# A decoder layer in fp32: its first stages laid out by scan step and tiled by columns

## The reference, cut to what matters

```python
xB = jnp.einsum('bsd,de->sbe', x, Bm)
h_final, _ = jax.lax.scan(lambda h, u: (h @ A + u, None), h0, xB)      # 256 steps
h_proj = h_final @ W_imp.T
importance = softmax(einsum('bsd,bd->bs', x, h_proj))
token_pref = softmax(einsum('bsd,nd->bsn', x, W_router))
neuron_w = einsum('bs,bsn->bn', importance, token_pref)
neuron_w = neuron_w / (neuron_w.sum(-1, keepdims=True) + 1e-08)
shared_compress = einsum('bn,ndr->bdr', neuron_w, compress)
Q = einsum('bsd,bdr->bsr', x, shared_compress)
scores = einsum('bsr,nr->bsn', Q, K) / sqrt(128)
# then: top 8 of 8192 scores per token, gather of V rows, their weighted sum, layernorm;
# cross-attention (16 heads), layernorm; a switched expert layer, layernorm
```

## Time and profile before

| | us |
|---|---|
| median of 3 runs (lowest to highest) | 1506.57 (1502.82 to 1507.38) |
| the profiled execution: its own time | 1504.98 |
| its span, first to last instruction | 1503.1 |
| PE, DVE, ACT, POOL busy | 1384.4, 1077.7, 736.7, 728.4 |
| mean granted TensorE clock | 0.968 |

### The profile page before, as it was taken

One profiled execution on the slowest core, in us unless ns is written; L12 is line 12 of the kernel. 1 busy time (PEld: TensorE's weight loads), 2 busy tenths in 40 slices (PEclk: granted clock), 3 DMA queues, 4 the chain that ended last, 5 costly groups with the idle time before them and its releaser, 6 DMA issues.

```text
span 1503.1 us, 25372 instructions
## 1 busy us (share of the span) xinstructions
PE 1384.4 (92%) x9840; PEld 1009.9 (67%) x9840; DVE 1077.7 (72%) x1626; ACT 736.7 (49%) x1381; POOL 728.4 (48%) x1010
## 2 busy tenths in 40 slices
PE   6986859999999999999999999999999988568998
PEld 2631648586877778686868777786868667356765
DVE  2110899978888888879788888888797862037567
ACT  2213435555555564646555555646465532315455
POOL 4400223747465564656474655656565753530225
PEclk9988889999999999999999999999999999879999
DMA  7316211213121212222131212122221311152313
GB/s 267 117 57 199 60 46 53 65 53 96 46 71 50 68 50 71 65 67 70 51 96 48 70 50 68 50 73 65 64 60 55 82 36 31 35 192 87 114 61 124
DMA packets 66759, 115.82 MB, mean 77 GB/s; under 512 B 10576, under 2 KB 44240, under 8 KB 66512
## 3 DMA queue, kind: packets, MB, share of 16 engines
q1 hardware_dynamic: 49200, 63.69, 14.7%
q0 software_dynamic: 14848, 41.96, 9.4%
q10 hardware_dynamic: 2592, 8.56, 1.7%
HBM read 103.42 MB, written 10.75 MB: 76 GB/s over the span
## 4 chain that ended last, share of the span: by engine, by line
PE 80%; DVE 13%; DMA 3%; issue 2%; POOL 1%; ACT 1%; SPq 1%; POOLq 0%; DVEq 0%; ACTq 0%
PE proj_bank L355 38%; PE score_bank L355 28%; PE sim_bank L355 10%; DVE cand_idx L948 3%; DVE cand_val L947 3%; DVE x_sum L971 2%; PE score_bank L641 2%; DMA comp_stage<-in_comp 1%; PE sim_bank L641 1%; DVE dispatchedT L1085 1%; PE sim_bank L575 1%; POOL exp L1170 1%; POOL v_rows L1141 0%; PE sim_bank L465 0%; DMA x_pair<-x_scratch 0%
## 5 line engine op out<-in xcount | busy, mean ns | idle before, releaser
L1141 POOL DMA_INDIRECT v_rows<-in_V,top_idx x256 | 248.2, 970 | 299.8 <-DVE top_idx L961 217.6
L727 ACT COPY score_row<-score_bank 128x512 f32<-128x512 f32 x512 | 298.5, 588 | 175.5 <-PE score_bank L355 103.0
L947 DVE MAX8 cand_val<-score_row 128x8 f32<-128x2048 f32 x128 | 292.2, 2282 | 103.7 <-ACT score_row L727 103.7
L1170 POOL TENSOR_SCALAR exp<-exp,exp_bound 128x256 f32<-128x256 f32 x512 | 246.9, 499 | 143.4 <-ACT exp L739 142.7
L948 DVE FIND_INDEX8 cand_idx<-cand_val,score_row 128x8 uint32<-128x2048 f32 x128 | 292.5, 2285 | 0.0
L355 PE MATMUL score_bank<-keysT_hi,qT_hi 128*128 128x512 f32 x512 | 219.5, 429 | 26.0 <-ACT score_row L727 25.0
L355 PE MATMUL score_bank<-keysT_lo,qT_hi 128*128 128x512 f32 x512 | 205.5, 401 | 0.0
L355 PE MATMUL score_bank<-keysT_hi,qT_lo 128*128 128x512 f32 x512 | 205.4, 401 | 0.0
L739 ACT ACTIVATE exp<-sim_bank 128x512 f32<-128x512 f32 x256 | 139.0, 595 | 113.8 <-PE sim_bank L355 113.8
L355 PE MATMUL sim_bank<-qT_heads,kT 64*128 64x256 f32 x1024 | 145.8, 403 | 7.7 <-ACT exp L739 7.7
L971 DVE SCALAR_TENSOR_TENSOR x_sum<-v_rows,top_weight,x_sum 128x256 f32<-128x256 f32 x256 | 134.7, 526 | 13.4 <-DMA v_rows<-in_V,top_idx 4.3
(11 more groups left out here) (168 smaller groups left out, 2301.3 us busy)
## 6 DMA issues: line engine op xcount, KB each, us to landing
kT<-den_scratch SPq DMA_DIRECT2D x64, 256.0 KB, 4.0
comp_stage<-in_comp SPq DMA_DIRECT2D x32, 256.0 KB, 3.7
x_pair<-x_scratch SPq DMA_DIRECT2D x32, 256.0 KB, 2.8
f_quads<-in_f POOLq DMA_DIRECT2D x32, 256.0 KB, 5.2
stage<-in_KmT ACTq DMA_DIRECT2D x8, 512.0 KB, 4.5
xT_all_<-in_xT SPq DMA_DIRECT2D x4, 1024.0 KB, 9.8
xT_in<-in_xT SPq DMA_DIRECT2D x16, 256.0 KB, 3.7
x_sum<-in_x SPq DMA_DIRECT2D x32, 128.0 KB, 2.1
```

The source lines that it names most:

```text
L727: nc.scalar.copy(srow[n // PER % 2][:, i * CB:(i + 1) * CB], scb[n % 3]).then_inc(sem("score_evac"), 1)
L947: own(nc.vector.max(cv[:, tile, cs], srow[g % 2][:, :]))
L1141: pool.indirect_dma_start(out=vg[:, k, :], out_offset=None, in_=V_rows, in_offset=bass.IndirectOffsetOnAxis(ap=i8[:, tile, k:k + 1], axis=0))\
L1170: last = nc.gpsimd.tensor_scalar(ex[i % NEX][:, k, :], ex[i % NEX][:, k, :], ub[:, k, c:c + 1], E_LO, ALU.min, ALU.max)
```

## The change

It rebuilds the head and leaves the order of the turns as it was, but for the weights' split.

1. **x by scan step.** A second input `xTs` holds x transposed and its tokens reordered: half of the 16 steps, sequence, step, and innermost the 16 groups, so that the moving operand of scan1 has runs of 16 elements (64 bytes); importance and router read 128 elements in a run. `xTa` becomes `xs`, of the same 4 MB.
2. **Column tiles.** scan1's two halves of D go to PSUM rows 0 to 63 and 64 to 127 (`qw`, A^T and the copies become 128 wide for that). Importance goes to four groups of 32 rows, the compression too: four 512-column products side by side in one bank, so its result is 8 copies of 128x512 (by ACT and DVE in turn) instead of 32 of 32x512, and 8 stores of 256 KB instead of 32 of 64 KB. The neuron weights take `uwd` (16 columns, diagonal) as stationary and 64 moving columns; their sum is then a DVE reduction and not a product.
3. **The compression's input ahead.** All 8 MB of `comp` are loaded at the start, in eight loads of 1 MB, into the space where `kl`, `wh`, `wl` stand later and two buffers.
4. **Order.** The router's four groups are spread between the powers and the scans. SP loads `xt` and `sct` of sequence 0 without waiting on `main_ready`. ACT copies `ba`.
5. **Keys split in place.** `KmT` is loaded whole into `kraw` (ACT issues it after x has landed), `kl` is written over its space. Wq, Wk, Wv are loaded by SP after `sct`; ACT copies them in the turn c = -2 between score copies, POOL subtracts them before its first gather, TensorE waits for them before the first `V` product.

```diff
+        "xTs": tiled(x.T).reshape(P, KT, B, RAD, TT, 8).transpose(0, 1, 4, 2, 5, 3).reshape(P, KT, TT, B, P),
...
-                last = mm(scp[r % 2][0:SD, 512:512 + SD], src[:, n, :], tpw[r][:, :])
+                if r < 7:
+                    last = mm(scp[r % 2][0:SD, 512:512 + 2 * SD], src[0:SD, n, :], tpw[r][:, :])
...
-                    last = mm(pp[0][0:SD, 0:B * RAD], ba[:, k, RAD - 1 - i, :],
-                              xTa[:, k, :].rearrange("p (n i) -> p i n", i=RAD)[:, i, :],
-                              start=(i == 0 and k == 0), stop=(i == RAD - 1 and k == KT - 1))
+                    last = mm(pp[0][k * SD:(k + 1) * SD, 0:B * RAD], ba[:, k, RAD - 1 - i, :],
+                              xs_step[:, k, i // 8, i % 8, :, :], start=(i == 0), stop=(i == RAD - 1))
...
-            for b in range(B):
+            for j in range(4):
                 for k in range(KT):
-                    last = mm(pp[0][0:B, 0:S], hm[:, k, b, :], xTa[:, k, b * S:(b + 1) * S],
-                              start=(b == 0 and k == 0), stop=(b == B - 1 and k == KT - 1))
+                    for c in range(4):
+                        b = 4 * c + j
+                        last = mm(pp[0][32 * c:32 * c + 32, 0:S], hm[:, k, b, :],
+                                  xs[:, k, :, b, :],
+                                  start=(j == 0 and k == 0), stop=(j == 3 and k == KT - 1))
...
-                    last = mm(pp[0][0:NC, b:b + 1], rte[:, g, :], uw[:, g:g + 1], start=(t == 0), stop=(t == TT - 1))
+                    last = mm(pp[0][0:B, 0:NC], uwd[:, t, b * B:(b + 1) * B], rte[:, t * B + b, :],
+                              start=(t == 0 and b == 0), stop=(t == TT - 1 and b == B - 1))
...
-                mm(sc_bank[n % 4][0:B * KT, :], nd[:, :, :].rearrange("p b k -> p (b k)"),
-                   cst[n % 5][:, :]).then_inc(sem("comp_used"), 1)
+                for c in range(4):
+                    last = mm(bank4[32 * c:32 * c + 32, g % 4, :], nd[:, :, :].rearrange("p b k -> p (b k)"),
+                              comp_at[g][:, c * 512:(c + 1) * 512])
+                last.then_inc(sem("sc_pe"), 1)
...
+                    if c == -2 and j < 3:
+                        weight_hi(2 * j)
+                        weight_hi(2 * j + 1)
...
             pool.wait_ge(sem("main_ready"), 1)
+            for n, (w, i, k) in enumerate(WCHUNKS):
+                pool.wait_ge(sem("w_hi"), n + 1)
+                nc.gpsimd.tensor_tensor(wl[:, i, k, :], wraw[:, 1, i, k, :], wh[:, i, k, :].bitcast(F32),
+                                        ALU.subtract).then_inc(sem("w_lo"), 1)
```

More of the change, by code:

```diff
@@ L23 @@
 TOPK = 8
-STW = 1024
+KW = 1024
 H, DH = 16, 64
@@ L38 @@
 E_LO, E_HI = float(np.exp(np.float32(-5.0))), float(np.exp(np.float32(5.0)))
-PRE_PE = {k: n + 1 for n, k in enumerate(("scan1", "scan2", "hproj", "imp_pe", "impT_pe", "nw_pe", "nws_pe"))}
+PRE_PE = {k: n + 1 for n, k in enumerate(("scan1", "scan2", "hproj", "imp_pe", "impT_pe", "nw_pe", "nwT_pe"))}
 PRE_DVE = {k: n + 1 for n, k in enumerate(("scan1_evac", "scan2_evac", "hm_evac", "imp_max", "imp_sm", "uw_done",
-                                           "nw_evac", "nd_done"))}
+                                           "nw_done", "nd_done"))}
+NG_SC = 8
 CB = 512
@@ L291, in _ @@
[L291 to L294, removed]
+                h, bs = q // 2, slice(q % 2 * 8, q % 2 * 8 + 8)
+                sp.dma_start(xs[:, :, h, bs, :], xTs[:, :, h, bs, :]).then_inc(sem(f"xs_in{q}"), 16)
+            for g in range(NG_SC):
+                sp.dma_start(comp_at[g], comp[:, g * CH:(g + 1) * CH]).then_inc(sem(f"comp_in{g}"), 16)
@@ L361, in mm3, with power @@
                 return mm(o, ll, rh, start=False, stop=last)
-            pe.wait_ge(sem("small_in"), 16 * 7)
-            for r in range(8):
+            def power(r):
                 if r:
@@ L380, in _, with router @@
                    pw[:, 8 * hf:8 * hf + 8, :].rearrange("p a b -> p (a b)")).then_inc(sem("ba_pe"), 1)
+            def router(n):
+                h, b0 = n // 2, n % 2 * 8
+                for b in range(8):
+                    for k in range(KT):
+                        last = mm(rt_bank[n][:, b * NC:(b + 1) * NC], xs[:, k, h, b0 + b, :],
+                                  wrt[:, k, :], start=(k == 0), stop=(k == KT - 1))
+                last.then_inc(sem("router_pe"), 1)
+            pe.wait_ge(sem("A_in"), 32)
@@ L381, in _ @@
+            for r in range(4):
+                power(r)
+            pe.wait_ge(sem("bmt_in"), 16)
+            pe.wait_ge(sem("small_in"), 16 * 6)
+            power(4)
+            bm_power(0)
+            power(5)
+            bm_power(1)
+            power(6)
+            bm_power(2)
+            pe.wait_ge(sem("xs_in0"), 16)
+            router(0)
+            power(7)
+            bm_power(3)
+            pe.wait_ge(sem("xs_in1"), 16)
+            router(1)
             pe.wait_ge(sem("ba_evac"), 4)
-            pe.wait_ge(sem("xTa_in"), 16 * 5)
+            pe.wait_ge(sem("xs_in2"), 16)
@@ L916, in _ @@
-            after("nw_chain", nc.vector.tensor_scalar(nw[:, 1, :], pp[1][0:NC, 0:B], 1e-8, None, ALU.add), 1)
-            after("nw_chain", nc.vector.reciprocal(nw[:, 2, :], nw[:, 1, :]), 2)
+            for t in range(TT):
+                last = nc.vector.tensor_tensor(
+                    uwd[:, t, 0:B * B:B + 1].rearrange("p (c j) -> p c j", j=4),
+                    rrc[:, t * B:(t + 1) * B].rearrange("p (c j) -> p c j", j=4),
+                    sp_[1][:, t * P:(t + 1) * P].rearrange("p (c m) -> p c m", c=4)[:, :, 0:4], ALU.mult)
@@ new lines, in _ @@
+            last.then_inc(sem("pre_dve"), 1)
+            dve.wait_ge(sem("pre_pe"), PRE_PE["nw_pe"])
+            after("nw_chain", nc.vector.tensor_reduce(nws[:, 0:1], pp[0][0:B, 0:NC], AX, ALU.add), 1)
+            after("nw_chain", nc.vector.tensor_scalar(nws[:, 1:2], nws[:, 0:1], 1e-8, None, ALU.add), 2)
+            after("nw_chain", nc.vector.reciprocal(nws[:, 2:3], nws[:, 1:2]), 3)
+            for o in range(2):
+                last = nc.vector.tensor_scalar(nwd[:, o, :], pp[0][0:B, 0:NC], nws[:, 2:3], None, ALU.mult)
```

266 lines of the change are left out of this document (138 added, 128 removed).

## The result

| | before | after |
|---|---|---|
| median, us (lowest to highest) | 1506.97 (1502.82 to 1511.49) | 1467.53 (1463.96 to 1468.99) |
| ratio to before, 95% interval | | 0.9727 (0.9702 to 0.9753) |
| the profiled execution: its own time / span | 1504.98 / 1503.1 | 1467.52 / 1465.7 |
| first score product starts | 150.19 | 109.58 |
| from there to the end of the span | 1352.9 | 1356.1 |

The kernel is 2.7% faster, 39 us. I had forecast 63: 1443.4, with a range from 1435 to 1458, so the result lies outside. Nearly all of the difference sits in the head. The first score product came at 109.58 where I had put 86.0, so 23.6 of the 24.1 us are there. What follows it got 3.2 us longer, where I had taken 1. (The two add up between the profiled executions: 1441.8 forecast, 1467.52 measured, 25.7 us apart, of which 23.6 in the head and 2.2 behind it. The medians are 24.1 apart.)

A forecast was written before the change was run, and what follows sets the result against it. The head, one chain, bounds the kernel: the first score product comes at 86.0 instead of 150.2, 64.2 us less; minus 1 in the turns, 63.2 less. Forecast 1443.4 us; 1435 to 1449 at 64%, 1435 to 1458 some 85%.

The forecast's parts named there:

- the store 1.6 (a quarter megabyte, so I take 2.0): Head's tail: after one more copy of 0.7, the compressed matrix's store takes 2.0 us.
- the rival: TensorE's clock stays low in the head (routers, power 7, neuron weights, compression): 6 to 15 us more, 1449 to 1458; 15%.
- here the clock decides: Router 0 to router 1: 4 us of router 0 at the lower level, 5.6 us in all; router 1 ends at 35.2.
- The rival's figure of 42 for the end of router 1: Head: if the clock stays down to the end of router 1, that end comes at 42 instead of 35.2.
- The neuron weights: Head, behind importance: 64 passes with 64 moving columns take 5.0 us, bounds 4.0 and 6.8.
- the compression: Head: 64 passes of 512 columns in four tiles take 10 us, some 4 us first at the lower level, without waiting for loads.
- A^T: Start of the head: A^T, issued at 1.4, takes 4.7 us to load, so the powers start at 6.1 instead of 7.96.
- Layout and column tiles: Head: scan1 at 0.1175 a pass, 7.5 us, despite runs of 64 bytes; importance in four tiles 4.0 instead of 15.3.
- The weights in the turns: First turns: weight copies fit ACT's idle time; POOL's subtractions make the first gather late, 1 us, bounds 0 and 3.
- the keys' rests: POOL: last four subtractions follow ACT's copies at 59 to 63 and end near 70, 13 us ahead of need.
- `x_sum` of the first tile: Sign in the turns: it waits for `v_rows` for at most 3 us.
- The turns as a block: Turns and expert part are shifted as a block, as long as before to 3 us; otherwise the forecast is wrong.

The follow-up runs named there:

- e1: Changed kernel with its 8 stores of 256 KB shaped 32x4x512 instead of 4x32x512: 1456.23 us, ratio 0.9645.
- e2: Changed kernel with all four router groups behind scan1 and ahead of scan2: 1460.10 us, ratio 0.9681.
- e4: Changed kernel with e1 (as 16 stores of 32x2x512), e2 and e3 together: 1442.09 us, ratio 0.9564.
- e6: e4 with scan1's moving operand read at the old 64-byte step, column tiles kept, output not the reference's: 1448.03 us, ratio 0.9623.
- e7: e4 with importance's four column tiles all sent to PSUM rows 0 to 31, output not the reference's: 1453.83 us, ratio 0.9658.
- e5: e4 with 64 more rows of zeros under Bm^T and the powers, so `ba` contracts over 128 rows: 1446.02 us, ratio 0.9598.
- e8b: e5 with powers 4 to 7 first, then the four products of `ba` in a run: 1439.94 us, ratio 0.9578.
- e9b: e4 with the order of e8b and no zero rows, as control: 1447.19 us, ratio 0.9624.
- e3: Changed kernel with the last two of POOL's six weight subtractions behind the first gather: 1463.44 us, ratio 0.9705.

## Why the prediction was wrong

**Where the bound lay: right.** The head is one chain, and all that it gave up ahead of the first score product the kernel gave up. e1, e2, e4, e6 and e7 moved that product by -9.9, -9.0, -23.6, +3.7 and +10.3 us (the last two against e4) and the medians by -11.3, -7.4, -25.4, +5.9 and +11.7. The product's figures are from one execution each, with the 1.5 us that an execution can differ by.

**The step that failed first: "the store 1.6 (a quarter megabyte, so I take 2.0)".** The 1.58 of the earlier trace rows was one store of 32x512, with 32 as its outermost dimension and 31 others long gone. I scaled its bytes and not its shape, and I took the last store alone where eight are queued. Measured 18.8 us. e1 shows the shape to be worth 11.7 of it, e4 with smaller stores 14.3; 4.5 us stay, so 2.0 was too small even for the best stores tried. This one term is 16.8 of the 24.1 us, and it was outside the bounds, since I had given it none.

**The clock: the rival was right in its first half, and it was to have 15%.** At "here the clock decides" I took 4 us of router 0 at the lower level, from the rises 2.4 and 5.1 us into dense stretches of the earlier trace rows. Those stretches were products of 256 and 512 columns. Router groups load weights as long as they stream, and powers, `ba` and two router groups without a gap (12.86 to 40.17 in the chain of after, 27 us) did not raise the clock; scan1 did, some 3 us in. The row that said so was in my own text, `ba`'s dense 7.13 us at the lower level, and I gave it too little weight against the earlier trace rows. The rival's figure of 42 for the end of router 1, against 35.2, was close: 40.17. What neither I nor the rival had priced is that the fall behind scan2 takes router 3 and the start of importance with it: router 3 took 3.4 us more. In sum +6.4, +1.6, +4.0 and +1.4. The neuron weights and the compression, which the rival had at the lower level too, were spared. e2 gives 9.0 us back by order alone. e5, e8b and e9b show that more than TensorE's being occupied is behind it.

**What was better.** A^T landed after 2.17 us, not 4.7; why, I did not test. The neuron weights (3.76 against 5.0) and the compression (7.12 against 10, 0.111 a pass, the ideal of four tiles at the upper level) ran with the clock up from their first pass, since it had risen late in importance: together with the start -5.9 us. For the neuron weights that is luck of the execution. In e1 and e3, with the same code up to there, the clock fell again in between and they took 5.3 us, so the 5.0 of the forecast was fair.

**Layout and column tiles: right.** scan1 showed no cost of its runs of 64 bytes (0.117 a pass against 0.1175 of the earlier trace rows), and e6 gives the layout alone; four tiles ran side by side (e7). The compression did not wait for `comp`.

**The weights in the turns: the cost was too small, and on the wrong engine.** ACT copied them between score copies with no wait, SP's loads were in time, the keys' rests ended at 80.9 us (I had said near 70) and still 29 us ahead of the first score product, and `x_sum` of the first tile, at 153.4, had no wait. The cost is DVE's, 3.8 us by the durations, where I had taken 1, with bounds of 0 and 3, for a late POOL. I had counted for each engine what it does and not what two engines do to each other.

**The turns as a block: nearly.** First score product to first `top_idx` +3.7 us; first to last `top_idx` +2.6; last to the end of the span -3.0 (287.4 before, 284.4 after), in all +3.2. The last of these is no effect of the change: over the eleven kernels profiled here, with the same code there, it lies between 281.6 and 289.5. The 2.6 I can't explain. In the ten changed kernels this middle stretch takes 1042.1 to 1045.4 us, against 1039.9 in the one execution before. One place that differs is the last of ACT's four copies of the first `V` products, before and after:

```profile
237.99 0.59 ACT L744 COPY v<-proj_bank 128x512 f32<-128x512 f32 x1 [0.81 <-PE proj_bank L355]
```

```profile
203.14 0.59 ACT L789 COPY v<-proj_bank 128x512 f32<-128x512 f32 x1 [2.27 <-remote]
```

ACT is idle ahead of it for 2.27 us, and the profile doesn't name for what. e4 has the idle time too, 2.96 us, and e3 2.10. That is at most a part of the 2.6, and no run was made to test it.

## What to carry to other kernels

A DMA's price is that of its shape and of its place in a queue, not that of its bytes alone: look at the outermost dimension on both sides, and count all that is queued between the last producer and the last landing. When pieces of TensorE's work are moved, their price moves with the clock, and a stretch that keeps the clock up need not be one that raises it: put the long products first, and price each piece at both levels. Work that fits into an engine's idle time can still stop another engine: a VectorE operation with two inputs in SBUF and a GpSimd subtraction side by side are to be counted as one behind the other. And a better layout of the moving operand gave its factor of two only where the clock was up (e6).

## What the runs showed that I had not expected

- A granted clock of 1.00 in the record does not mean the upper level: up to about 43 us in the kernel after the passes ran at the lower level: the router group took 7.02 us under 1.00 and again 7.02 under 0.50, and 3.57 in e2.
- 13 us of TensorE without a gap (14.0 to 26.9 in e5, 8.0 us of it products on 128 rows and 512 columns) left the clock down, and so did 27 us in the kernel after (12.86 to 40.17); eight such passes in a run raised it (5.85 us), the same eight on 64 rows did not raise it within their 6.83.
- Two of DVE's operations went from 0.19 and 0.42 us to 1.75 and 2.65 beside POOL's subtractions of 2.4.
- Moving operands in runs of 64 bytes cost nothing over contiguous ones (0.117 us a pass against 0.1175); single elements 64 bytes apart cost a factor of two at the upper level, with and without column tiles (0.223 and 0.43), and nothing to be seen at the lower one.
- With the same code, the neuron weights took 3.76 us in the kernel after and 5.3 in e1 and e3, as the clock happened to stay up or fall.
- Stores of 256 KB as 4x32x512 ran at 110 GB/s, as 32x4x512 at 261.
